# Group order in the first attention, and weights of p+1, a pipelined preparation and weighing ahead of turning in the quantised one

## The reference

```python
q = (x @ Wq.T) in 32 heads; k, v from context
q, k = rmsnorm(q), rmsnorm(k)
attn = softmax(einsum('bhnd,bhmd->bhnm', q, k) * 8 ** -0.5)
out = einsum('bhnm,bhmd->bhnd', attn, v)
```

```python
q = x @ Wq + bq; kv = cond @ Wkv + bkv
q = fq_sym(q * scale, axis=-1); k = fq_sym(k, axis=-1); v = fq_sym(v, axis=keys)
attn = fq_unsigned(softmax(q @ k.T), axis=-1)      # s = max/255, round(x/s) in 0..255
out = (attn @ v) @ Wp + bp
```

## Time and profile before

| | us |
|---|---|
| median of 3 runs | 2033.98 |
| lowest and highest | 2030.72, 2037.86 |
| the profiled execution | 2037.22 |
| its span | 2035.4 |

### The profile page before, as it was taken

The page is one execution under the profiler, slowest core; times in us unless marked ns, Lnnn a source line. Parts: engine busy times, 40 slices in busy tenths (PEclk is TensorE's granted clock), DMA queues, the critical chain, the costliest instruction groups (busy, mean ns, idle before and its releaser), DMA issues.

```text
span 2035.4 us, 27127 instructions
## 1 busy us (share of the span) xinstructions
PE 1672.4 (82%) x9118; PEld 1167.4 (57%) x9138; DVE 1251.8 (62%) x2816; ACT 908.9 (45%) x2585; POOL 246.4 (12%) x447
## 2 busy tenths in 40 slices
PE   6996663897998998998599999638888889897876
PEld 5885442464665665666466776414454555675655
DVE  4457996577677677766224322368878888564342
ACT  2332221554554554554235533018878789232211
POOL 0000001232233333331000000000000000000000
PEclk8887775999999999999699989765555555896889
DMA  5102001000000000000500000000000000100000
GB/s 211 78 3 83 0 0 44 1 3 4 1 3 3 1 2 4 1 1 1 218 1 1 0 0 0 8 8 1 1 0 0 0 0 1 42 0 0 1 0 21
DMA packets 13578, 38.01 MB, mean 19 GB/s; under 512 B 2201, under 2 KB 8866, under 8 KB 10802
## 3 DMA queue, kind: packets, MB, share of 16 engines
q1 hardware_dynamic: 13490, 36.99, 4.8%
HBM read 35.94 MB, written 1.05 MB: 18 GB/s over the span
## 4 chain that ended last, share of the span: by engine, by line
PE 53%; DVE 28%; ACT 7%; issue 6%; POOL 4%; DMA 1%; DVEq 0%; POOLq 0%; ACTq 0%; SPq 0%; another core or an unknown queue 0%
PE PS L1106 7%; PE PS L2402 3%; PE PS L1784 3%; PE PS L1764 3%; DVE small L1907 2%; PE PS L1516 2%; POOL small L1005 2%; PE PS L1472 2%; PE PS L350 2%; PE PS L362 2%; PE PS L1159 2%; PE PS L1179 2%; ACT work L1847 2%; PE PS L1451 2%; DVE work L1917 2%
## 5 line engine op out<-in xcount | busy, mean ns | idle before, releaser
L1106 PE MATMUL PS<-late,spare 128*128 128x512 f32 x384 | 181.5, 610 | 27.9 <-DVE spare L922 24.8
L1784 PEld LDWEIGHTS PS<-ident_b,work 128*128 128x128 bf16 x1024 | 97.4, 140 | 148.8 <-DVE work L1917 124.8
L1907 DVE TENSOR_REDUCE small<-PS 128x1 f32<-128x1024 f32 x128 | 156.4, 1222 | 25.0 <-PE PS L1764 19.5
L1079 ACT ACTIVATE work<-PS,small 128x128 f32<-128x128 f32 x256 | 90.6, 366 | 177.1 <-DVE small L943 177.1
L1784 PE MATMUL PS<-ident_b,work 128*128 128x128 bf16 x1024 | 130.6, 308 | 39.5 <-DVE work L1917 31.4
L1847 ACT ACTIVATE work<-PS,small 128x1024 f32<-128x1024 f32 x128 | 155.1, 1212 | 11.3 <-DVE small L1909 11.0
L1840 ACT COPY work<-PS 128x1024 bf16<-128x1024 bf16 x128 | 129.6, 1012 | 38.8 <-PE PS L1784 38.3
L199 POOL TENSOR_TENSOR rstd<-moments,eps 128x1 f32<-128x1 f32 x56 | 10.6, 189 | 1068.6 <-DVE moments L179 1068.6
L1764 PE MATMUL PS<-early,work 64*128 64x512 bf16 x256 | 129.9, 609 | 1.9 <-ACT work L1847 1.8
L1106 PEld LDWEIGHTS PS<-late,spare 128*128 128x128 f32 x384 | 70.9, 195 | 102.5 <-issue 80.3
L1190 PE MATMUL PS<-late,work 128*128 128x256 f32 x512 | 125.4, 389 | 1.6 <-DVE work L894 1.6
(11 more groups left out here) (357 smaller groups left out, 3679.4 us busy)
## 6 DMA issues: line engine op xcount, KB each, us to landing
late<-in_C_proj SPq DMA_DIRECT2D x1, 4096.0 KB, 12.0
ctxT<-in_ctxT SPq DMA_DIRECT2D x24, 128.0 KB, 2.5
late<-in_C_q SPq DMA_DIRECT2D x1, 2048.0 KB, 8.9
late<-in_C_qx SPq DMA_DIRECT2D x1, 2048.0 KB, 13.1
late<-in_F_w SPq DMA_DIRECT2D x2, 1024.0 KB
late<-in_B_gate SPq DMA_DIRECT2D x1, 1024.0 KB, 8.8
late<-in_B_up SPq DMA_DIRECT2D x1, 1024.0 KB, 10.5
late<-in_B_down SPq DMA_DIRECT2D x1, 1024.0 KB, 12.4
```

The costliest lines, as they stand in the source:

```text
L1079: last = nc.scalar.activation(C_[g]["p"][:, h, :], PS[:, SBANK, h * P:(h + 1) * P], ACT.Exp, scale=DC ** -0.5, bias=small[:, g, 8 + h:9 + ...
L1106: last = nc.tensor.matmul(PS[:, n, :], src(k), w[:, k, c0:c0 + 512], start=k == 0, stop=k == KC - 1)
L1784: last = nc.tensor.transpose(bank(g, 1).bitcast(BF16)[:, b * P:(b + 1) * P], E_[g]["pb"][:, b * P:(b + 1) * P], ident_b[:])
L1907: ch.link(nc.vector.tensor_reduce(small[:, g, 80:81], banks(g, 2), AX.X, ALU.max))
```

## The change

In the first attention `scores` and `weigh` have the loops swapped: m outside, j inside, so that each matmul is in another row or column group than the one ahead of it. The waits for ACT's exponentials are drawn together: one for all four ahead of a block. The scores' flags of all four banks come in the last round.

In the quantised attention:
- `whole` subtracts MAGIC - 1 in place of MAGIC, so the integers are 1 to 256 and the copy `p_T` can move two bf16 as one f32. The sum of v over the keys, made once by 8 matmuls of ones with `E_vq` in `weigh` of unit 0, is subtracted from each result (one more DVE operation for a batch).
- The preparation is unrolled over the 8 batches: DVE rounds batch b (`rounded_k`), then takes the third part of batch b-2 and the second remainder of b-1; the two casts are ACT's (`high`, `middle`); step 0's norm, x and q stand between. The k stack has a place of its own, and bank 2 of each half is used for turning it. ctx's buffers are released by DVE's reading.
- Scaling and rounding of v (`E_values`) move from ahead of the pipeline to slot 2 of it, on DVE.
- PE's order in a slot becomes extra, scores, weigh, turn.

The flags of the first attention are used again for the new ones. The diff, cut to its core:

```diff
@@ scores and weigh of the first attention
-                for j in range(4):
-                    if r:
-                        pe.wait_ge(A_exp.sem, A_exp.nth(i, 4 * r - 4 + j))
-                    rows = slice(32 * j, 32 * j + DA)
-                    for m in range(4):
+                if r:
+                    pe.wait_ge(A_exp.sem, A_exp.nth(i, 4 * r - 1))
+                for m in range(4):
+                    for j in range(4):
+                        rows = slice(32 * j, 32 * j + DA)
                         last = nc.tensor.matmul(PS[:, j, m * P:(m + 1) * P], A_[g]["kT"][rows, 4 * half + m, :],
                                                 A_[g]["qT"][rows, 4 * half + m, :], start=True, stop=True)
-                    last.then_inc(A_scores.sem, 1)
+                        if m == 3:
+                            last.then_inc(A_scores.sem, 1)
...
-                for j in range(4):
-                    pe.wait_ge(A_exp.sem, A_exp.nth(i, 4 * r + j))
-                    for m in range(4):
+                pe.wait_ge(A_exp.sem, A_exp.nth(i, 4 * r + 3))
+                for m in range(4):
+                    for j in range(4):
                         last = nc.tensor.matmul(PS[32 * j:32 * j + 32, 4 + half, m * P:(m + 1) * P],
                                                 A_[g]["v1"][:, 4 * half + m + TA * j, :], A_[half]["p"][:, j, m, :], start=True, stop=True)
@@ preparation, PE
+            def project_kv(b):
+                g = b % G
+                ctx_loaded(pe, b // G, g)
+                if b >= G:
+                    pe.wait_ge(E_kvread.sem, E_kvread.nth(0, b - G))
...
+            def turn_kstack(b):
+                g = b % G
+                pe.wait_ge(E_kstack.sem, E_kstack.nth(0, b))
+                if b >= G:
+                    pe.wait_ge(E_kTs.sem, E_kTs.nth(0, b - G))
...
+            for b in range(NB + G):
+                if b < NB:
+                    project_kv(b)
+                if b >= G:
+                    turn_kstack(b - G)
+                if b == 1:
+                    for g in range(G):
+                        E_turn_x(pe, 0, g)
+                if b == 2:
+                    for g in range(G):
+                        E_project_q(pe, 0, g)
+                if b in (4, 5):
+                    E_turn_stack(pe, 0, b - 4)
+            pe.wait_ge(E_kTs.sem, E_kTs.nth(0, NB - 1))
@@ preparation, ACT
+            for b in range(NB + G):
+                if b < NB:
+                    high(b)
+                if b >= G:
+                    k_T(b - G)
+                if 0 <= b - 1 < NB:
+                    middle(b - 1)
...
@@ preparation, DVE
+            norm_stats(ch, 0)
+            for b in range(NB + G):
+                if b < NB:
+                    rounded_k(b)
+                if b == NB - 1:
+                    nc.vector.tensor_reduce(E_vs[:, 1, :], E_v.rearrange("p b d -> p d b"), AX.X, ALU.max,
+                                            apply_absolute_value=True).then_inc(E_vmax.sem, 1)
+                if b >= G:
+                    less_middle(b - G)
+                if 0 <= b - 1 < NB:
+                    less_high(b - 1)
+                if b == 0:
+                    E_normed_x(dve, 0)
+                if b == 2:
+                    for g in range(G):
+                        E_read_q(dve, 0, g)
+                if b in (3, 4):
+                    E_quantised_q(dve, ch, 0, b - 3)
+                    E_switch(ch, 0, b - 3)
@@ pipeline
             def weigh(ch, i, u):
                 h, g = head_of(u), u % G
+                if u == 0:
+                    pe.wait_ge(prepared, PREPARED[4])
+                    for b in range(NB):
+                        last = nc.tensor.matmul(bank(1, 0)[:, D:2 * D], ones_b, E_vq[:, b, :], start=b == 0, stop=b == NB - 1)
+                    last.then_inc(E_vsummed.sem, 1)
+                if u == 1:
+                    pe.wait_ge(E_vsummed.sem, E_vsummed.nth(0, 1))
...
-            E_pipeline(pe, None, first, [(None, extra), (0, scores), (2, turn), (3, weigh)])
+            E_pipeline(pe, None, lambda ch: None, [(None, extra), (0, scores), (3, weigh), (2, turn)])
...
-                nc.scalar.copy(E_[g]["pT"].rearrange("p a b -> p (a b)"), bank(g, 1).bitcast(BF16)).then_inc(E_pT.sem, 1)
+                nc.scalar.copy(E_[g]["pT"].rearrange("p a b -> p (a b)").bitcast(F32), bank(g, 1)).then_inc(E_pT.sem, 1)
...
-                nc.vector.tensor_scalar(E_[g]["pb"], E_[g]["e"], MAGIC, MAGIC, ALU.add, ALU.subtract).then_inc(E_pb.sem, 1)
+                nc.vector.tensor_scalar(E_[g]["pb"], E_[g]["e"], MAGIC, MAGIC - 1.0, ALU.add, ALU.subtract).then_inc(E_pb.sem, 1)
...
+                if n == G:
+                    E_values(dve, ch)
+                if n == G + 2:
+                    dve.wait_ge(E_vsummed.sem, E_vsummed.nth(0, 0))
+                    nc.vector.tensor_copy(E_vsum, bank(1, 0)[:, D:2 * D]).then_inc(E_vsummed.sem, 1)
...
-                    ch.link(nc.vector.tensor_tensor(heads16(e["t"]), heads16(bank(b, 0)[:, 0:D]), over_d(small[:, b, 16:32]), ALU.mult))
+                    ch.link(nc.vector.tensor_tensor(e["t"], bank(b, 0)[:, 0:D], E_vsum, ALU.subtract))
+                    ch.link(nc.vector.tensor_tensor(heads16(e["t"]), heads16(e["t"]), over_d(small[:, b, 16:32]), ALU.mult))
```

More of the change, by code:

```diff
@@ L98, in step_flag, with follow @@
             return StepFlag(sem(name), per)
+        def follow(earlier, per=1):
+            f = Flag(earlier.sem, per)
+            f.base = earlier.base + NB * earlier.per
+            return f
         X = sb("X", [P, NB, D])
@@ L1627, in E_before_tensor @@
         def E_before_tensor(pe, ch):
-            pe.wait_ge(x_done.sem, 4 * NB)
[L1629 to L1642, removed]
@@ L1643, in E_before_tensor @@
-            pe.wait_ge(prepared, PREPARED[4])
-        def E_before_scalar(act, ch):
[L1646 to L1651, removed]
+            def project_kv(b):
[3 more added lines that the diff above has]
+                    pe.wait_ge(E_kvread.sem, E_kvread.nth(0, b - G))
+                for k in range(KC):
+                    last = nc.tensor.matmul(bank(g, 0), ctxT[:, g, k, :], wE["kv"][:, k, :], start=k == 0, stop=k == KC - 1)
+                last.then_inc(E_kv.sem, 1)
@@ L1660, in E_before_vector @@
             for g in range(G):
-                ch.mark(nc.vector.memset(E_[g]["stack"].rearrange("p a b c -> p (a b c)"), 0.0))
+                ch.mark(nc.vector.memset(E_[g]["kstack"][:, :, 3, :], 0.0))
+                ch.mark(nc.vector.memset(E_[g]["stack"][:, :, 3, :], 0.0))
+            ch.mark(nc.vector.memset(ones_b, 1.0))
             ch.restart()
[L1663 to L1683, removed]
@@ L1687, in E_before_vector, with E_values @@
+        def E_values(dve, ch):
             dve.wait_ge(E_vall, 1)
@@ L1858, in extra @@
                     nc.scalar.copy(E_[g]["oT"].rearrange("p a b -> p (a b)"), bank(g, 1)[:, 0:D]).then_inc(E_oTs.sem, 1)
-            def first(ch):
-                for part in (x_T, q_T):
-                    for g in range(G):
-                        part(0, g)
-            E_pipeline(act, ch, first, [(2, exps), (3, p_T), (None, extra)])
+            E_pipeline(act, ch, lambda ch: None, [(2, exps), (3, p_T), (None, extra)])
         def E_gpsimd(pool, ch):
@@ new lines, in E_gpsimd, with E_normed_x, E_read_q @@
+            E_pipeline(pool, ch, lambda ch: None, [(None, extra)])
+        def E_normed_x(dve, i):
+            for g in range(G):
+                dve.wait_ge(rstd_ready.sem, rstd_ready.at(i, g))
+                nc.vector.tensor_scalar(xn[:, g, :], X[:, i * G + g, :], moments[:, g, 0:1], rstd[:, g, :],
+                                        ALU.subtract, ALU.mult).then_inc(xn_ready.sem, 1)
+        def E_read_q(dve, i, g):
+            dve.wait_ge(E_q.sem, E_q.at(i, g))
+            nc.vector.tensor_tensor(E_[g]["t"], bank(g, 1)[:, 0:D], E_bias[:, 0:D], ALU.add).then_inc(E_qread.sem, 1)
@@ new lines, in E_quantised_q @@
+        def E_quantised_q(dve, ch, i, g):
+            e = E_[g]
+            dve.wait_ge(E_qread.sem, E_qread.at(i, g))
+            ch.link(nc.vector.tensor_scalar(e["t"], e["t"], DE ** -0.5, None, ALU.mult))
+            s, r = small[:, g, 96:112], small[:, g, 16:32]
+            step_of(ch, e["t"], s, r)
+            ch.link(nc.vector.tensor_tensor(heads16(e["u"]), heads16(e["t"]), over_d(r), ALU.mult))
+            for part in range(3):
+                last = nc.vector.tensor_scalar(e["stack"][:, :, part, :], heads16(e["u"]), MAGIC, MAGIC, ALU.add, ALU.subtract)
+            last.then_inc(E_qstack.sem, 1)
@@ L1941, in extra @@
                 if n == E_DEPTH + 2:
-                    normed_x(i + 1)
+                    E_normed_x(dve, i + 1)
                 if n in (E_Q + 3, E_Q + 6):
-                    quantised_q(ch, i + 1, (n - E_Q) // 3 - 1)
-            def first(ch):
-                norm_stats(ch, 0)
-                normed_x(0)
-                for g in range(G):
```

(7 more changed lines are left out.)

169 lines of the change are left out of this document (103 added, 66 removed).

## The result

The changed kernel takes 1997.39 us (median; 1996.82 to 1997.61), the kernel before 2033.35 on the same chip: a ratio of 0.9821, 95% interval 0.9809 to 0.9834. The forecast was 2012, so the kernel is 15 us faster than forecast. The profiled execution's span went from 2035.4 to 1995.0, 40.4 less, and the stages account for it. (The profiled execution of before stood 3.2 us over its median, that of after did not; by the medians the gain is 36.) Boundaries are the first maximum over 1024 columns in the part behind the first attention (L708 before, L715 after), the preparation's first DVE instruction, and the first and last maximum over the scores. The pipeline's "units" run from one of these maxima to the next.

The account below looks back on a forecast made before the run. PE was taken as busiest, with the largest part of the chain. First attention -10, preparation -14, values' scaling +7, pipeline -5 make -22: 2037.2 profiled becomes 2015, less 3.2 over the median, 2012 us; own range 2000 to 2024, overall 1990 to 2030.

Parts of the forecast that it names:

- Groups: First attention: alternating groups cuts scores from 2.75 to 1.8 us and weighing to 1.4; part -10 us (-23 to +15).
- The bound below of 0.8: First attention: least time in us for either block, from PE's closest spacing in the trace, 8 records in 0.20.
- The clock's charge: First attention: PE idles about 2 us per batch, so more stretches run at 1.2 GHz; 4 us charged (0 to 8).
- The hidden parts: First attention: second scores and first weighing save nothing beside DVE's 5.3 us; a batch saves 1.95 us.
- Preparation: From batch 3 each period is rounding, last part, turning, projection in series, 7.2 us; stage -14 us (-22 to -8).
- rival B: Preparation runs at DVE's pace, 5 x 3.8 us for 36, 17 less: 1995 us; chance 0.08.
- Scaling of the values: Pipeline start: uncovered 5.6 us hole after two units, plus some 1.7 us for summing values; +7 us (5 to 9).
- Copy, plain units, subtraction: Pipeline: copy 1.01 to 0.59 us, plain units 2.13 to 2.16 (-2.5 us in all), subtraction 0.46 in two units a step (+3.7).
- The pipeline's term: Pipeline of the quantised attention: copy, order and subtraction together give -5 us (-9 to +2), at granted clock 0.5.
- Weighing ahead of turning: Pipeline: fills PE's wait in long units, 0.20 us in 8 to 9 units of a step; -6 us.
- rival C: PE's clock rises in the pipeline; some 42 long units lose about 1 us each, 45 less: 1967 us; chance 0.05.

Follow-up runs that it names:

- filled_wait: The changed kernel plus two unread 512-column f32 matmuls per batch behind the first weighing of the first attention, in PE's wait for normalised q: 1984.05 us.
- project_ahead: The changed kernel with PE in the preparation projecting k and v of batch b+1 before turning batch b-2: 1979.89 us.
- turn_first: The changed kernel with PE's old order in the pipeline put back, turning ahead of weighing: 2011.11 us.
- no_plus_one: The changed kernel with weights p in place of p + 1, the sum still subtracted, so the output is not the reference's: 1995.05 us.
- bf16_copy: The changed kernel with ACT copying the turned weights as 1024 bf16 again, in the new order weigh, turn: 2008.68 us.
- turn_first_fill: The changed kernel with turning ahead of weighing and one unread 256-column f32 matmul in units with a q copy, stack or projection: 2014.82 us.

## Why the prediction was right, and where not

**Groups, right, sized low.** -13.2 against -10. Alternating groups pays, and more than "1.8" and "1.4": 1.10 and 1.0 us. The bound below of 0.8 was the nearer end: the prediction took two groups side by side, and the trace has all four. The Trainium skill ("TensorE: Matmul & The Clock Gate", section "Wait — 56ns, not 53.3ns?") has about 62 ns for a matmul with hardware decode off. The trace has 34 ns a record; counted over the 16 matmuls that the code writes it is 69, so the figure of the Trainium skill would have come near here if taken for those and not for the 32 records. The eight in 0.20 of the earlier trace rows stay below it either way.

**The clock's charge, right in kind, and too small.** "PE now idles about 2 us per batch", and the charge was 4. It idles 3.17 in six batches and 6.33 in the seventh, and pays for the two to four blocks behind it, 0.8 to 0.9 for a block: 1.6 to 2.9 a batch, some 15 in all, of which filled_wait gave back 13.3. A larger gain and a larger charge nearly met, and that the sum came near -10 is partly luck.

**The hidden parts, right for the batch that was read.** In the batch of the earlier trace rows the second scores and the first weighing give nothing: they lose 3.05 together, and PE's wait for DVE is 3.17. But that batch is the quickest of before, 16.72 us at a granted 1.00; the other five behind the first take 17.7 to 19.8. The next one takes 18.05 at 0.91, with PE busy for 17.96 of it, and its first weighing is slow:
```profile
111.62 3.80 PE L362 MATMUL PS<-work,spare 128*32 128x128 f32 x32
115.35 1.09 PE L336 MATMUL PS<-ident,work 128*128 128x128 f32 x8
```
PE turns q at once behind it, without waiting, so there DVE's 5.3 us are not what holds the batch, and a shorter first weighing counts. With the clock kept up, a batch goes from 16.72 to 13.70 in filled_wait: 3.0, where the prediction had 1.95.

**Preparation, right.** -16.2 against -14, and the named series (rounding, last part, turning, projection) is the one in the trace. The five periods from batch 2's rounding to batch 7's are 9.2, 6.2, 8.9, 7.9 and 7.9, together 40.1; the prediction had 36 for them and 4.2 for q's work on PE, which lies inside them: 40.2. The tail came as worked out too; the first batches went 1.6 sooner. project_ahead shows rival B's pace and what stands in its way: PE's order, as was said.

**Scaling of the values, right.** A hole after two units, where PE waits 5.20; +5.1 over the first units against +7. The hole costs 5.0; summing the values costs 0.7 and not 1.7; and three units behind, now at 2.4 GHz, give 0.6 back.

**Copy, plain units, subtraction, right.** 0.586; 2.15 for 2.13 to 2.16, though by the copy and the order together; the two units with the subtraction grew by 0.45 or a little more (2.78 to 3.25, 2.78 to 3.23), against 0.46.

**The pipeline's term, wrong in size.** "-5 (-9 to +2)" was -16.6. The step that failed is the assumption under it, that PE stays at the granted 0.5. Weighing ahead of turning saved 7 or 8 at that clock, for 6; another 9 or 10 came from long units that now run at 2.4 GHz and that the sum put at nothing. With the old order (turn_first) the cheap copy and the subtraction leave these units at 328.7, as before. That is rival C in part: its mechanism (units of 4 us losing over 1 us of PE) is what the rows show, in about 12 units and not in 42. The 1997.4 measured lies under the forecast's own range, 2000 to 2024; without this part it would be some 2007 (an estimate).

**Open.** Why this order raises the clock in just these units. The + 1 in the data (no_plus_one, 0.59) and the copy's speed (bf16_copy, 0.58) are excluded. That PE's idle time in the unit does it was argued from turn_first and tried in turn_first_fill, which moved the clock but not the time; so the mean clock answers to PE's work in the pipeline, but what places the fast stretches is not shown.

## What to carry to other kernels

Where PE has blocks of small matmuls on separate row or column groups, step through the groups in the inner loop, and then look at what PE waits for next: a wait of 3 us cost as much in the blocks behind it as the reordering of a block had gained, and two matmuls that nobody reads gave it back. In a software pipeline write down the series that one buffer goes through; here one line of order (project the next before turning the last) was worth 14 us with no work removed. A mean granted clock says nothing of time until it is known which units the fast stretches fall on.

## What the runs showed of the hardware that I had not expected

- 32 records of 8x128 or 128x32 f32 matmuls on four groups in turn take 1.10 and about 1.0 us; group after group, the same take 2.75 and 2.4.
- After an idle time of 3.2 us PE works at 1.2 GHz for the next two to four blocks (1.90 and 1.88 us in place of 1.09 and 1.08); with 1.25 us of idle time left, it doesn't. The clock also falls without any wait: in the batch of before from 103.14 us PE is busy for 17.96 of 18.05, and its first weighing is granted 0.60.
- With PE busy for 84 to 88% of its time, the pipeline is granted 0.52 to 0.61: a busy PE was no sign of a full clock.
- ACT's copy out of the matmul output memory goes by elements: the same bytes take 1.012 us as 1024 bf16 and 0.586 as 512 f32, and 256 elements take 0.37 or 0.38 in either type.
- The unchanged middle of the program takes 1091.9 to 1096.2 us over these kernels, 4 us for no edit in it, and the pipeline without an edit 337.6 to 343.1. What a stage gained has to be read in the stage.
